# Cross-attention, two-path feed-forward and routing on one core: the order of both walks dealt anew

## What is computed

```python
x = x + xattn(layernorm(x), ctx)     # 16 heads of 64, 64 keys per batch, biases, output bias
x = x + ffn(layernorm(x))
# ffn, dense: causal attention with 16 heads of 16; h = x + rmsnorm(o @ wo); silu(h @ w1) * (h @ w3) @ w2
# ffn, sparse: softmax router, the 2 best of 8 experts per token, each silu(x @ ew1) * (x @ ew3) @ ew2
# the sum of dense h + rmsnorm(ffn) and of rmsnorm(sparse) is added
```

## Time and profile before

| | before |
|---|---|
| median of 3 runs | 1550.32 |
| the three runs | 1542.5, 1551.01, 1550.32 |
| the profiled execution, its own time | 1540.53 |
| its span | 1538.8 |
| granted TensorE clock, mean | 0.966 |
| busy share of PE, DVE, ACT, POOL | 88%, 53%, 37%, 38% |

### The profile page before, as it was taken

How to read it: one execution, slowest core, us unless ns; L and a number is a source line. 1 busy time by engine, 2 the same in 40 slices (tenths; PEclk the granted TensorE clock), 3 DMA queues, 4 the chain that set the end, 5 groups by cost and what they waited for, 6 DMA issues and landing times. The chain is left out here.

```text
span 1538.8 us, 21916 instructions
## 1 busy us (share of the span) xinstructions
PE 1357.7 (88%) x6989; PEld 844.2 (55%) x6990; DVE 812.8 (53%) x1656; ACT 572.5 (37%) x1207; POOL 591.5 (38%) x1040
## 2 busy tenths in 40 slices
PE   6997759997999898989979997989899879999995
PEld 5443425663566366646745663566366536666664
DVE  2442554476447626853774486348536823333348
ACT  2334325402630452155125403531452253443446
POOL 4111224324432534254234324331634155555544
PEclk9998969998999999999999999999999999999998
DMA  6128530350043007100700340052005434332245
GB/s 206 48 97 255 202 98 1 92 142 15 1 125 110 15 1 198 43 8 28 206 16 1 110 125 15 1 157 77 15 4 144 128 100 127 127 99 86 89 169 200
DMA packets 82264, 141.61 MB, mean 92 GB/s; under 512 B 10632, under 2 KB 66336, under 8 KB 78720
## 3 DMA queue, kind: packets, MB, share of 16 engines
q1 hardware_dynamic: 62512, 94.37, 20.2%
q10 hardware_dynamic: 13184, 28.34, 6.3%
q0 software_dynamic: 6480, 17.77, 3.4%
HBM read 84.90 MB, written 55.15 MB: 91 GB/s over the span
## 5 line engine op out<-in xcount | busy, mean ns | idle before, releaser
L1325 ACT ACTIVATE room<-ps 128x512 f32<-128x512 f32 x320 | 180.5, 598 | 175.7 <-PE ps L1061 175.0
L1648 DVE TENSOR_REDUCE nm<-ps 128x2 f32<-128x256 f32 (+3 forms) x256 | 200.2, 819 | 82.2 <-PE ps L1035 80.5
L1116 PE MATMUL ps<-hT,w 128*128 128x512 f32 x768 | 207.5, 414 | 0.0
L731 POOL TENSOR_SCALAR_AFFINE_SELECT room<-room 128x256 f32<-128x256 f32 (+1 forms) x320 | 119.8, 384 | 148.7 <-ACT room L1325 146.2
L1116 PEld LDWEIGHTS ps<-hT,w 128*128 128x128 f32 x768 | 141.5, 192 | 34.0 <-DVE hT L1678 2.0
L1034 PE MATMUL ps<-room 96*128 96x128 bf16 (+3 forms) x512 | 125.0, 312 | 32.1 <-DMA room<-parts_d 16.0
L965 PE MATMUL ps<-room,xnT 128*128 128x512 f32 x256 | 131.9, 640 | 20.7 <-ACT xnT L1211 14.5
L1061 PE MATMUL ps<-room 99*128 99x384 bf16 (+3 forms) x512 | 113.0, 310 | 29.5 <-ACT room L1325 26.9
L1152 PE MATMUL ps<-room 128*128 x284 | 135.4, 599 | 1.9 <-ACT room L1375 1.9
L1347 ACT ACTIVATE room<-ps 128x512 f32<-128x512 f32 x64 | 37.2, 592 | 267.5 <-PE ps L1116 267.5
L1126 PE MATMUL ps<-w,room 128*128 128x256 f32 x512 | 129.4, 392 | 8.1 <-DVE room L1699 8.1
(11 more groups left out here) (245 smaller groups left out, 2265.4 us busy)
## 6 DMA issues: line engine op xcount, KB each, us to landing
room<-parts_d SPq DMA_DIRECT2D x48, 256.0 KB, 9.8
room<-parts_d ACTq DMA_DIRECT2D x48, 256.0 KB, 7.4
room<-xs_d SPq DMA_DIRECT2D x71, 129.0 KB, 2.1
parts_d<-room SPq DMA_DIRECT2D x64, 128.0 KB, 1.8
vw_d<-stage ACTq DMA_DIRECT2D x8, 1024.0 KB, 4.4
room<-pair_d SPq DMA_DIRECT2D x8, 1024.0 KB, 8.0
m_d<-stage ACTq DMA_DIRECT2D x8, 896.0 KB, 5.6
room<-m_d SPq DMA_DIRECT2D x7, 1024.0 KB, 5.1
```

The costliest lines, as they stand in the source:

```text
L731: done(g.affine_select(out=w, in_=w, compare_op=ALU.is_ge, fill=0.0, base=0, pattern=[[0, 2]] * (blocks - 1) + [[1, P]], channel_multiplie ...
L1116: last = mm(bank(up_banks(b, m)[i]), w[:, x, k, m * P:(m + 1) * P], hT[:, y, k, :], start=((x, y, k) == terms[0]), stop=((x, y, k) == term ...
L1325: done(fn(prob[:, u * 512:(u + 1) * 512], bank(score_bank(b) + n % 2), ACT.Exp), "b_exp")
L1648: done(v.tensor_reduce(nm[:, t, 2 * hp:2 * hp + 2], pair_ps, AX.X, ALU.max, negate=True), "a_max")
```

## The change

1. `STEPS` (walks 2 to 8) and `FIRST_WALK` are written out as literal lists, each with the same steps as before, 205 and 162, in another order.
2. A value fold's two halves were both copied by ACT (`vf`, two of L1253). Now ACT copies one and DVE the other. `vp` writes banks 6 and 7 in turn, and no longer only 6.
3. `load_kv` is split. For batch 1 the keys are loaded ahead of the shifts, once the `m_out` stores are in; the values behind the shifts, once all `vw_out` stores are in. `cv` waits for the values, `cs` for the keys alone.
4. Once, in walk 1: DVE's turning of `wq` and `wk` stands at `ct.2.0` and no longer at `qk.0`, and POOL's count for `bq` uses another semaphore.

No instruction is added or removed besides this: 16 of ACT's L1253 become DVE's.

```diff
-    x_in=16, kv_in=64, stats=4, stats1=1, mv1=1, rstd1=1, xn1=1, xT1=2, xnT=2, bq=1,
+    x_in=16, kv_in=32, stats=4, stats1=1, mv1=1, rstd1=1, xn1=1, xT1=2, xnT=2, vw_in=32,
-FIRST_ONLY = ("bq", "m_ps", "m_act", "m_dve")
+FIRST_ONLY = ("m_ps", "m_act", "m_dve")
+LATER_ONLY = ("vw_in",)
...
-STEPS = interleaved() + TAIL
+def dealt(text):
+    return [(w[0], *map(int, w[1:])) for w in (word.split(".") for word in text.split())]
+FIRST_WALK = dealt("""
...
+    max.4.0 vp.6 max.4.1 vf.5.0 max.4.2 max.4.3 vf.5.1 shift.0 max.5.0 max.5.1 vf.6.0 nx_stats vp.7 max.5.2 max.5.3 max.6.0 vw_out.3 vf.6.1 vw_out.4
+    max.6.1 max.6.2 max.6.3 vf.7.0 nx_apply max.7.0 max.7.1 vf.7.1 max.7.2 vw_out.5 vw_out.6 max.7.3 vw_out.7 shift_parts.1 z w_split
+""")
+STEPS = dealt("""
+    x_turn.0 x_turn.1 cs.0.0 sc.0.0 sc.0.1 cs.0.1 sc.0.2 sc.0.3 shift.1 sc.0.4 sc.0.5 cs.1.0 sc.0.6 sc.0.7 va.0.0 exp.0 sc.0.8 sc.0.9 sum.0 cs.1.1
+    sc.1.0 sc.1.1 va.0.1 sc.1.2 sc.1.3 va.0.2 sc.1.4 ct.0.0 sc.1.5 cs.2.0 sc.1.6 sc.1.7 ct.0.1 out_t.0 sc.1.8 sc.1.9 va.1.0 va.1.1 exp.1 sc.2.0 x_bias
...
...
-            def load_kv(n):
+            def load_keys(n):
                 need(sp, n - 1, "sc_ps", T)
                 need(sp, n - 1, "sc_add", T)
-                need(sp, n - 1, "pv_ps", T)
                 done(sp.dma_start(m_next, m_d[n, :, :, :]), "kv_in", 16)
                 done(sp.dma_start(bqk_next, bqk_d[n, :, :].rearrange("h k -> (h k)").partition_broadcast(P)), "kv_in", 16)
+
+            def load_values(n):
+                need(sp, n - 1, "pv_ps", T)
                 for j in range(2):
                     done(sp.dma_start(vw_next[j * CK:(j + 1) * CK, :, :],
-                                      vw_d[n // 2, n % 2, :, :, :].rearrange("k (a j) m -> k a j m", j=2)[:, :, j, :]), "kv_in", 16)
+                                      vw_d[n // 2, n % 2, :, :, :].rearrange("k (a j) m -> k a j m", j=2)[:, :, j, :]), "vw_in", 16)
...
                         need(sp, b, "rep_q", per["rep_q"])
                         need(sp, b, "rep_k", per["rep_k"])
                         sp.sem_inc(freed, 1)
-                        load_kv(b + 1)
-                    send_shifts(b, 0)
+                        load_keys(b + 1)
+                        load_values(b + 1)
                     if c is None:
                         for i in range(2):
                             sp.wait_ge(m_out[i], 16 * KD * PAIRS // 4)
                         sp.wait_ge(p0["bqk_out"], 16)
+                        sp.sem_inc(freed, 1)
+                        load_keys(b + 1)
+                    send_shifts(b, 0)
+                    if c is None:
                         for i in range(4):
                             sp.wait_ge(kv_out[i], 16 * PAIRS // 4)
                         sp.sem_inc(freed, 1)
-                        load_kv(b + 1)
+                        load_values(b + 1)
...
+                        to = 6 + step[1] % 2 if kind == "vp" else 6
+                        if i == 0:
+                            pe.wait_ge(sems["kv_in"], per["kv_in"])
+                        elif i <= PAIRS:
                             pe.wait_ge(p0["kv_sb"], i)
                         else:
-                            pe.wait_ge(sems["kv_in"], 64)
+                            pe.wait_ge(p0["kv_sb"], i - 1)
+                        if i == PAIRS + 1:
+                            pe.wait_ge(p0["fold_act"], 2 * PAIRS + 1)
                         w = wk_c if kind == "kp" else wv_c
                         for k in range(KD):
-                            last = mm(bank(6), w[:, k, step[1] * P:(step[1] + 1) * P], ctxT[:, k, :], start=(k == 0), stop=(k == KD - 1))
+                            last = mm(bank(to), w[:, k, step[1] * P:(step[1] + 1) * P], ctxT[:, k, :], start=(k == 0), stop=(k == KD - 1))
...
-                        if f == 0:
-                            pe.wait_ge(p0["fold_dve"], 2 * PAIRS)
+                        pe.wait_ge(p0["fold_dve"], 2 * PAIRS + f)
...
+                        if half == 0 and t == 0 and c is not None:
+                            pe.wait_ge(sems["vw_in"], c * per["vw_in"] + per["vw_in"])
...
-                        for j in range(2):
-                            last = fn(vw_stage[pa % 4][:, half * 2:half * 2 + 2, j * D:(j + 1) * D], bank(4 + j).rearrange("p (c m) -> p c m", m=D), ACT.Copy)
-                        last.then_inc(p0["fold_act"], 1)
+                        fn(vw_stage[pa % 4][:, half * 2:half * 2 + 2, 0:D], bank(4).rearrange("p (c m) -> p c m", m=D), ACT.Copy).then_inc(p0["fold_act"], 1)
                     elif kind == "vw_out":
                         pa = step[1]
                         act.wait_ge(p0["fold_act"], 2 * PAIRS + 1 + 2 * pa + 2)
+                        act.wait_ge(p0["fold_dve"], 2 * PAIRS + 2 * pa + 2)
                         act.dma_start(vw_d[:, :, :, 2 * pa:2 * pa + 2, :].rearrange("c b k j m -> (b k) c (j m)"), vw_stage[pa % 4]).then_inc(kv_out[pa % 4], 16)
...
+                    elif kind == "vf":
+                        pa, half = step[1:]
+                        dve.wait_ge(p0["fold_ps"], 2 * PAIRS + 2 * pa + half + 1)
+                        if half == 0 and pa < 4:
+                            dve.wait_ge(m_out[pa // 2], 16 * KD * PAIRS // 4)
+                        elif half == 0:
+                            dve.wait_ge(kv_out[pa % 4], 16)
+                        v.tensor_copy(vw_stage[pa % 4][:, half * 2:half * 2 + 2, D:], bank(5).rearrange("p (c m) -> p c m", m=D)).then_inc(p0["fold_dve"], 1)
...
+                    elif step == ("ct", 2, 0) and c is None:
+                        dve.wait_ge(p0["w_late"], 16 * 9)
+                        for i, w in enumerate((wq, wk)):
...
```

112 lines of the change are left out of this document (34 added, 78 removed), and 8 rows, old and new, of tables (CROSS_FIRST, TAIL).

## The result

The changed kernel takes 1460.26 us (median of 4 runs, 1450.99 to 1462.2) beside 1546.9 us of the kernel before on the same chip: a ratio of 0.9428, 95% interval 0.9376 to 0.948. The gain is 86.6 where 54 was forecast (1496). The direction and the places were right and the size was short: the time lies outside the forecast's own 1474 to 1515, and only 0.3 inside the lower end of the whole range of 1460 to 1535. The profiled execution of after took 1460.08 us (span 1458.3), that of before 1540.5, so the two profiles differ by 80.4.

What follows compares the result with a forecast made beforehand. PE sets the pace, so an order returns only its idle: −7.0 per walk (−49) and −5.4 before walk 2 take 1540.5 to 1486.1; 9.8 carried over gives 1496. Own range 1474 to 1515, whole range 1460 to 1535.

Steps and rivals of the forecast that it cites:

- Head of the walk: Start of walks 2 to 8: 8.1 of PE's waits and lengthening go, 1.0 kept for ACT and POOL, gain 7.1.
- Projections: Projection stretch of each walk: a new PE wait of 1.3 at f_h_turn, while the 1.2 before fd goes.
- The wait for the replicas: Before each walk's first maximum: PE waits 2.2 instead of 2.8; nothing booked, range −2 to +2.
- The maxima: End of each walk: PE's part falls by 2.6 to 35.5, idle stays 1.95; nothing booked, −1 to +2.
- Better packing: Rival: maxima lose half their idle, replicas all covered; −10 per walk, −8 at walk 1, 1472; chance 0.15.
- Walk 1: First walk: maxima start at 142 instead of 153.4, then DVE bounds; last fold copied at 178.6, ends 175 and 198.
- Between walks 1 and 2: Pause before walk 2: stores 10, loads 12.5, split and turn 4.8; first score at 206.4 instead of 211.79, −5.4.
- The early keys are hidden: Pause before walk 2: loading the keys early is hidden, since w1 and w3 still land last.
- The clock: Idle before walk 2: same lower clock, nothing added; rival, one more lengthening of 1.2 per walk, 1537, chance 0.03.
- POOL beside DVE: POOL passes beside DVE's subtractions: at worst DVE loses 3.3 per walk, off PE's path; inside the −3 end.
- The slower rival: Rival at walk 2's first score: last fold at 198, stores in series, score at 232.5, +20.7; 1578, chance 0.05.
- The signs: Marks of being right: walks 133 to 138, waits on two lines under 2, maxima 36 to 39, last store near 178.

Runs made afterwards that it cites:

- exp_back: Changed kernel with exp.0 alone moved back to right behind cs.0.1; 1508.49 us, ratio 0.9747.
- old_exp_ct: old_exp with ct.0.0 and ct.0.1 also moved later, behind sc.1.2 and sc.1.3; 1507.82 us, ratio 0.975.
- old_exp: Changed kernel with the old STEPS, in them exp.0 and sum.0 moved behind sc.0.7 and ct.0.0 behind sc.0.8; 1540.86 us, ratio 0.9947.
- head_only: Changed kernel with the new STEPS up to cv.3.1 and the old order behind it, from norm_3 on; 1460.09 us, ratio 0.942.
- hb_bias_back: Changed kernel with POOL's f_hb set back behind cs.0.1 and x_bias behind sum.0; 1460.42 us, ratio 0.9429.
- proj_back: Changed kernel with the projections set back: f_o_norm behind qk.1, v.0 and v.1 behind qk.3, f_h_turn behind v.1, fu.0.0 behind v.3; 1458.32 us, ratio 0.941.
- max_pos: Changed kernel with fu.3.1 and fd.2.0 moved from ahead of max.0.0 to behind it; 1476.68 us, ratio 0.9527.
- max_more: Changed kernel with w1 and w3 loaded early, walk 1's last value folds moved up, and fg.3.1 and fu.4.0 ahead of max.0.0; 1427.0 us, ratio 0.9225.
- old_two: old_exp with fu.3.1 and fd.2.0 also moved ahead of max.0.0; 1527.9 us, ratio 0.9863.
- keys_late: Changed kernel with SP's load_keys(1) back directly ahead of load_values(1), behind the last store; 1465.11 us, ratio 0.9466.
- old_first: Changed kernel with the old list for walk 1 alone; 1463.78 us, ratio 0.9464.
- wup_early: Changed kernel with SP loading w1 and w3 ahead of the first shifts, and ACT's w_split waiting for the eight stores itself; 1445.63 us, ratio 0.9343.

## Why the prediction was right in its places and short in size

**Head of the walk: the term that was mis-sized.** The mechanism was right. The waits named in the earlier trace rows went, with the throttled scores behind them, and exp_back brings them back. The step read "I let go 8.1 … I keep 1.0 for both. Gain 7.1"; the head gave 10.3 in walk 4 and 10.6 in the mean. Two parts of it failed.
- "I keep 1.0" for ACT and POOL being late next: 0.2 at L1290 is all that came, and no wait on L691. Idle fell by 6.8, of the 6.9 (3.4, 2.6 and 0.88) that I had let go.
- "PE sets the pace, its work does not change, and an order can give back only what PE idles." The busy time of the same 372 matmuls fell by 3.5, where 1.18 was booked. Of the 3.5 some 1.7 is half clock: before has 0.50 for 3.4 us behind the wait, with PE busy throughout (the line below), of which I had counted the four L965 alone. The other 1.8 is overlap between neighbours that 11 more waits had broken (16 for 5, short ones counted), 0.16 each, as in old_exp_ct. Over seven walks, 7 × (1.0 + 0.5 + 1.8) = 23, added to the 49 that were forecast, makes 72; 73.7 was measured. The sum passes over that the half clock differs from head to head.

```profile
516.91:520.32 3.41, 3.41 (x9) 1.34 (x8) 0.97 (x2) 0.57 (x2) 3.12 (x2) 0.50 0.00 0
```

**What made the head short.** I had tied it to `exp` and to POOL coming late out of `z`. exp_back shows `exp`'s place to be necessary, old_exp that it is not enough, old_exp_ct that its reader has to go back with it, head_only that the deal as a whole gives the rest. Which of the other moves the last 7 belong to is open. POOL's `f_hb` and `x_bias` have 1.0 per walk of it in the new order (hb_bias_back).

**Projections.** New wait 1.3 forecast at `f_h_turn`; 1.63 in two pieces (1.06 and 0.57) for 0.75 before. The 1.2 before `fd` went. As forecast, they about cancel (proj_back).

**The wait for the replicas.** Forecast 2.2; measured 2.42:

```profile
550.70 3.72 ACTq L1281 DMA_DIRECT2D room<-parts_d  x6
554.58 4.63 SPq L524 DMA_DIRECT2D room<-parts_d  x6
...
567.09 0.22 PE L1000 MATMUL ps<-room 96*128 96x128 bf16 x1 [2.42 <-DMA room<-parts_d]
```

In this walk the size is right by two errors that cancel: the key issue comes 8.2 behind the end of `qk.3` where I had 5.6, and the maximum 12.5 behind the key issue where I had 16.0. In the other five walks the key issue does come 5.6 behind, and in the mean of the six it is 6.0 and 14.9, 20.9 in all for the 21.6 of the forecast. What the working had wrong is the mark it counted from. proj_back has the key issue back at its old place and its first maximum no sooner; it follows the first query replica, 16.6 in after and 16.5 in before, and the working named the `tanh` ahead of that issue but gave a later issue no price. That work put ahead of this wait is free and work behind it is not holds (max_pos, max_more); the 2.6 of it in the change is what the maxima lost, as forecast, and what the stretch ahead grew by. So it bought nothing here beside head_only, since the replicas went out 2.3 later; in old_two, where they went out as before, the same work ahead of the maximum gave 13 us.

**The maxima.** Booked nothing beside the 2.6 that moved; walk 4 has 37.20 for 40.0. Their idle is 1.46 for 1.95. "Better packing" (1472) was nearest in size of the rivals and wrong in mechanism: neither did the maxima lose half their idle nor were the replicas covered. It takes max_more for the second.

**Walk 1.** The maxima start at 136.53 instead of the forecast 142, with PE waiting 4.42 for the replicas; 5 us sooner than I had put it together (134.9 to 141.1 in the ten profiles with this walk 1); how much of that is the last key projection and how much the transfers was not taken apart. DVE is busy 35.01 of 41.70 there, or 0.84, where I had 33 at nine tenths. ACT makes its last fold copy at 175.75, DVE at 176.57, forecast 178.6: the later pace is paid by the earlier start. The split of the copies between ACT and DVE was not undone by itself.

**Between walks 1 and 2.** Right nearly term by term, forecast first: stores 10 and 9.8 (177.34 to 187.15), loads 12.5 and 12.7, split and first turn 4.8 and 4.8, first score at 206.4 and 204.87, idle 25 and 24.92. "The early keys are hidden" is to be read with the sum, which had 18.7 for 4.5 MB fall to 12.5 for 3 MB: their landing is hidden, and their bytes no longer stand ahead of `w1` and `w3`. keys_late shows that this is what they are worth, 17.1 for 12.7.

**The clock.** Forecast as no change. From the first score of walk 2 to the last maximum it is 0.50 for 45.7 us in before, 33.4 in after, 79.5 in exp_back and 10.8 in max_more. In after it is still 0.50 for 3.4 to 6.8 us behind the first maximum in some walks and at the first scores of others. One such stretch of walk 3:

```profile
436.20:439.60 3.40, 3.40 (x10) 2.76 (x9) 2.19 (x3) 0.49 (x1) 2.48 (x4) 0.50 0.84 316
```

A walk with such a stretch behind the first maximum has maxima of 38.2 to 38.4 (39.5 in walk 2, where it lasts 6.8), one without 36.8; a head with one has 57.6, one without 55.9. Behind the first maximum it stands in four of seven walks, and the length of the wait does not tell in which: it is there behind 1.96 and not behind 2.97. With the wait shortened (max_more) it is left in two of seven, with the wait lengthened (max_pos) it is there in seven. By the Trainium skill, TensorE: Matmul & The Clock Gate, HAM oscillation, idle gaps between groups let the clock fall; the runs agree, and exp_back is the case where it cost most (4.75 of idle, 6.9 in all). In which walk the clock falls behind a wait of 1.2 to 3.0 the runs leave open. The forecast had cited this rule only against the change; it works for it as well.

**POOL beside DVE.** DVE's subtraction takes at most 2.065 after, 2.056 before, the median 1.226 in both, and all 32 together 46.0 and 45.7. In before the ones above 2.0 have 0.96 to 0.98 us of POOL's `f_hb` pass (L739) beside them, in after 0.97 to 0.99 of its scaling (L709): one collision left and another came. In hb_bias_back they are beside the `f_hb` and the `x_bias` pass, and all 32 together take 53.8:

```profile
L1525 DVE TENSOR_TENSOR room<-room,cmax x32: 1224/1426/2978, 45.2 to 1045.7; 128x1024 f32<-128x1024 f32 x32
```

The longest have 1.9 us of the `x_bias` pass (L704) beside them. The contention that the Trainium skill's GPSIMD Engine Reference, Specifications, warns of is there in all three traces; the change did not make it grow.

**The slower rival** needed a last fold at 198. It came at 176. old_first, where walk 1 ends at 198.56, does not try this rival: its last store is issued at 180.69.

**The signs.** PE's waits on L1290 and L691 (0.2 and none in every walk), the wait on `parts_d` (2.0 to 3.0), the last store at 177.34 and the idle before walk 2 are as the prediction said; the maxima are 36.8 to 39.5 for 36 to 39. "No L965 of 3.17" holds in walks 3, 4 and 8 alone: in walks 5 to 7 the first four scores take 3.3 to 3.6, behind the waits of `x_turn`. Walks 3 to 8 take 131.4 to 135.5 for 133 to 138, which is the missing size again.

## What to carry to other kernels

When an order is changed so that PE no longer waits, book more than the listed idle: add some 0.16 us for each wait that goes, since neighbouring matmuls overlap again, and all of the half-clock stretch behind the wait, not its first matmuls alone. A producer and its reader have to be moved together; moved alone, the producer's wait turns up at the reader (old_exp). Where the page shows one fixed wait per pass on a transfer, put PE's work ahead of it until the wait is gone, and see that this does not put off the first issue of the transfers (old_two against the change); and in a queue ask of every transfer which data it needs, since two loads that stood behind stores they did not need cost 15 us (wup_early).

## What the runs showed of the hardware that was not expected

- Successive matmuls overlap by 0.16 to 0.18 us in the records, and busy time grows when waits break the overlap: 62.34 for 58.84 on the same 372 matmuls, 1.7 of it from the clock and 1.8 from 11 waits.
- A single wait of 4.75 us of PE cost 6.9 per walk, since the granted clock was 0.50 for 6.8 us from within the wait on (exp_back): four scores took 3.73 for 1.88.
- Of three stores of 1 MB issued within 1.5 us the first landed 4.3 behind its issue (175.81 to 180.09), the last 9.8 behind its own (177.34 to 187.15).
- DVE's subtraction of 128x1024, 1.22 by itself, takes 2.05 to 2.07 where POOL's scaling of 128x1024 runs beside it for 0.97 to 0.99 (after), and up to 2.98 beside 1.9 of POOL's `x_bias` pass (hb_bias_back).
